# Expert layer of a routed feed-forward stage: second product with the expert's weights as the loaded operand, and a turn of its result on TensorE

## The reference

```python
def _L1_ffn_ref(hidden_states, gate_w, gate_b, w1, w3, w2):
    x = hidden_states.reshape(T, D)
    probs = jax.nn.softmax((x @ gate_w + gate_b).astype(jnp.float32), axis=-1)
    top_w, top_idx = jax.lax.top_k(probs, TOP_K)
    top_w = top_w / jnp.sum(top_w, axis=-1, keepdims=True)
    combine = combine.at[jnp.arange(T)[:, None], top_idx].set(top_w)
    h = jax.nn.silu(jnp.einsum('td,edf->tef', x, w1)) * jnp.einsum('td,edf->tef', x, w3)
    out_e = jnp.einsum('tef,efd->ted', h, w2)
    out = jnp.einsum('ted,te->td', out_e, combine)
```

## Time and profile before

| | us |
|---|---|
| three runs | 1422.41, 1417.07, 1421.33 |
| median | 1421.33 |
| profiled execution | 1421.32 |
| its span | 1419.4 |
| mean granted clock of TensorE | 0.896 of full speed |

### The profile page before, as it was taken

One profiled execution on the slowest core, in us unless ns is written; L12 is line 12 of the kernel. 1 busy time (PEld: TensorE's weight loads), 2 busy tenths in 40 slices (PEclk: granted clock), 3 DMA queues, 4 the chain that ended last, 5 costly groups with the idle time before them and its releaser, 6 DMA issues. The chain is left out here.

```text
span 1419.4 us, 16931 instructions
## 1 busy us (share of the span) xinstructions
PE 1132.3 (80%) x5006; PEld 565.5 (40%) x5006; DVE 1013.0 (71%) x1416; ACT 785.3 (55%) x1269; POOL 725.3 (51%) x611
## 2 busy tenths in 40 slices
PE   4664689999999888888898889896684678777764
PEld 1221234444444333333333333332233567566563
DVE  4996775666645379999999999999927545444454
ACT  5664545646554468676777768584343333333344
POOL 0122351323312038887978888877621465565554
PEclk8775899999999989999999999999986788888885
DMA  6000000000000001000000000000001011111214
GB/s 209 0 0 0 0 2 0 1 1 0 0 0 1 0 30 30 15 16 15 15 16 15 30 0 0 0 0 1 0 9 52 27 40 41 38 39 40 41 41 171
DMA packets 13849, 33.25 MB, mean 23 GB/s; under 512 B 3568, under 2 KB 3760, under 8 KB 13552
## 3 DMA queue, kind: packets, MB, share of 16 engines
q1 hardware_dynamic: 8784, 22.10, 4.7%
q0 software_dynamic: 4992, 10.23, 2.7%
HBM read 23.01 MB, written 9.31 MB: 23 GB/s over the span
## 5 line engine op out<-in xcount | busy, mean ns | idle before, releaser
L1617 POOL TENSOR_TENSOR prod<-hs,csb 128x1024 f32<-128x1024 f32 x128 | 302.0, 2360 | 179.4 <-DVE hs L1667 178.5
L1667 DVE TENSOR_TENSOR_SCAN hs<-dA,carry,pD 128x512 f32<-128x512 f32 x256 | 313.9, 1268 | 5.5 <-DVE pD L1682 0.8
L1425 PE MATMUL pY<-prod,const 128*128 128x512 f32 x512 | 245.2, 601 | 11.3 <-DVE h L1652 7.4
L1532 ACT ACTIVATE dA<-dt,negA 128x512 f32<-128x512 f32 x256 | 169.9, 715 | 1.4 <-DVE dt L1719 1.4
L2388 DVE SCALAR_TENSOR_TENSOR hid<-pR,silu 128x512 f32<-128x512 f32 x78 | 53.9, 691 | 136.3 <-ACT silu L2099 97.4
L1425 PEld LDWEIGHTS pY<-prod,const 128*128 128x128 f32 x512 | 96.5, 192 | 122.3 <-issue 107.7
L1543 ACT ACTIVATE csb<-pC 128x512 f32<-128x512 f32 x128 | 76.0, 594 | 108.2 <-PE pC L1438 107.9
L2165 POOL DMA_INDIRECT moe_outs<-y,to x78 | 82.0, 1052 | 91.9 <-ACT y L2091 76.0
L2099 ACT ACTIVATE silu<-pR 128x512 f32<-128x512 f32 x78 | 46.5, 596 | 132.3 <-remote 66.7
L2145 POOL DMA_INDIRECT g<-moe_rows,source x78 | 80.3, 1029 | 48.9 <-DVE source L2337 25.5
L1878 PE MATMUL pR<-x,moe_hi 128*128 128x256 f16 x312 | 94.8, 304 | 12.1 <-issue 5.7
(11 more groups left out here) (398 smaller groups left out, 2719.5 us busy)
## 6 DMA issues: line engine op xcount, KB each, us to landing
raw<-moe_w SPq DMA_DIRECT2D x12, 512.0 KB, 3.6
room<-moe_outs SPq DMA_DIRECT2D x8, 512.0 KB, 7.5
X<-xT SPq DMA_DIRECT2D x4, 512.0 KB, 4.6
hidw<-hid_w SPq DMA_DIRECT2D x1, 2048.0 KB, 10.0
moe_rows<-xt SPq DMA_DIRECT2D x8, 256.0 KB, 2.0
outT<-X SPq DMA_DIRECT2D x8, 256.0 KB, 2.0
g<-moe_rows,source POOLq DMA_INDIRECT x78
moe_outs<-y,to POOLq DMA_INDIRECT x78
```

Of the source, the lines that this page charges most:

```text
L1425: last = nc.tensor.matmul(YB[c][:], G.ident, prod[:, slot(b, n), c, :], start=n == 0, stop=n == DST - 1)
L1532: last = nc.scalar.activation(dA[:, slot(b, n), c, :], dt[:, b, c, :], ACT.Exp, scale=negA[:, c, n:n + 1])
L1617: nc.gpsimd.tensor_tensor(prod[:, slot(b, n), :, :], hs[:, slot(b, n), :, :], csb[:, slot(b, n), :, :].to_broadcast([P, CB, N]), ALU.mult)\
L1667: last = nc.vector.tensor_tensor_scan(hs[:, slot(b, n), c, :], dA[:, slot(b, n), c, :], dBu(n, c), carry[:, b, n, c:c + 1], ALU.mult, ALU.add)
```

## The change

`down` uses the helper `product`, with the expert's weights as the loaded operand and all 256 rows moving: 6 matmuls of 256 columns per unit where there were 12 of 128. The result has channels on partitions, in the lower half of the bank. ACT copies it with the scale 1/WS to a new tile `y_by_channel` of 32-bit numbers (`take_y`), PE turns it by two matmuls of 128 columns against the 32-bit identity into the upper half of the bank (`y_turn`), and ACT copies that to `y` (`put_y`). `take_y(i - 2)` stands where `put_y(i - 2)` stood; `y_turn(i - 2)` and `put_y(i - 2)` come one unit later, `y_turn` between `up` and `down`. The ring of gathered tiles is 6 in place of 8, with `AHEAD` still 6.

```diff
@@ down, on PE
                 for h in range(2):
                     m = slice((2 * u + h) * P, (2 * u + h + 1) * P)
-                    w_hi, w_lo = of_expert(w2_hi, e, m), of_expert(w2_lo, e, m)
-                    for r in range(2):
-                        out = Y[:, i % 2, r * P:(r + 1) * P]
-                        at = slice(h * ROWS + r * P, h * ROWS + (r + 1) * P)
-                        nc.tensor.matmul(out, hid_hi[:, n % HR, at], w_hi, start=u == 0 and h == 0 and r == 0, stop=False)
-                        nc.tensor.matmul(out, hid_hi[:, n % HR, at], w_lo, start=False, stop=False)
-                        last = nc.tensor.matmul(out, hid_lo[:, n % HR, at], w_hi,
-                                                start=False, stop=u == 1 and h == 1 and r == 1)
+                    at = slice(h * ROWS, (h + 1) * ROWS)
+                    last = product(Y[:, i % 2, 0:ROWS], of_expert(w2_hi, e, m), of_expert(w2_lo, e, m),
+                                   hid_hi[:, n % HR, at], hid_lo[:, n % HR, at], u == 0 and h == 0, u == 1 and h == 1)
                 last.then_inc(S["down"], 1)
+            def y_turn(i):
+                pe.wait_ge(S["y_in"], i + 1)
+                for r in range(2):
+                    last = nc.tensor.matmul(Y[:, i % 2, ROWS + r * P:ROWS + (r + 1) * P],
+                                            y_by_channel[:, i % 2, r * P:(r + 1) * P], G.ident, start=True, stop=True)
+                last.then_inc(S["y_turned"], 1)
@@ the loop on PE
+                if u == 1 and i >= 2:
+                    y_turn(i - 2)
                 if n >= LAG:
                     down(n - LAG, es[(n - LAG) // 2])
             for n in range(UNITS - LAG, UNITS):
                 down(n, es[n // 2])
+                if n == UNITS - 2:
+                    y_turn(TILES - 2)
+            y_turn(TILES - 1)
@@ ACT
+            def take_y(i):
+                act.wait_ge(S["down"], 2 * i + 2)
+                if i >= 2:
+                    act.wait_ge(S["y_turned"], i - 1)
+                nc.scalar.activation(y_by_channel[:, i % 2, :], Y[:, i % 2, 0:ROWS], ACT.Copy, scale=1.0 / WS)\
+                  .then_inc(S["y_in"], 1)
             def put_y(i):
-                act.wait_ge(S["down"], 2 * i + 2)
+                act.wait_ge(S["y_turned"], i + 1)
...
                 if u == 0 and i >= 2:
+                    take_y(i - 2)
+                if u == 1 and i >= 2:
                     put_y(i - 2)
             hid_high(UNITS - 1)
             act.preload_act_table_set("natural_log_exp_and_others")
-            put_y(TILES - 2)
-            put_y(TILES - 1)
+            for i in (TILES - 2, TILES - 1):
+                take_y(i)
+                put_y(i)
```

More of the change, by code:

```diff
@@ L1744, in phase_moe @@
     GRID = B * T // ROWS
-    AHEAD, GR, HR, YR = 6, 8, 4, 4
+    AHEAD, GR, HR, YR = 6, 6, 4, 4
     SOON, LATE = 16, COLS - 16
@@ L1815, in phase_moe @@
         y = sb("y4", [P, YR, 2, P])
+        y_by_channel = sb("y_by_channel4", [P, 2, ROWS])
         w13_hi, w13_lo = G.moe_hi[:, 0:E, :], G.moe_lo[:, 0:E, :]
@@ L1845, in phase_moe @@
                  "past expert_f expert hot_col hot_part hot_pair hot_low listed row_f empty second from_f to source "
-                 "gathered0 gathered1 gathered2 gathered3 gathered4 gathered5 gathered6 gathered7 scattered0 scattered1 scattered2 scattered3 x_turned x_in up silus hidden hid_high hid_low down y_out "
+                 "gathered0 gathered1 gathered2 gathered3 gathered4 gathered5 scattered0 scattered1 scattered2 scattered3 x_turned x_in up silus hidden hid_high hid_low down y_in y_turned y_out "
                  "back0 back1 back2 back3 back4 back5 back6 back7 summed minus squaredC weighted logC rstdC scale scaledC turnedC addedC stored").split()
@@ L2085, in hid_high @@
                 nc.scalar.activation(hid_hi[:, n % HR, :], hid[:, n % HR, :], ACT.Copy).then_inc(S["hid_high"], 1)
+            def take_y(i):
[4 more added lines that the diff above has]
+                  .then_inc(S["y_in"], 1)
             def put_y(i):
-                act.wait_ge(S["down"], 2 * i + 2)
+                act.wait_ge(S["y_turned"], i + 1)
                 if i >= YR:
                     act.wait_ge(S[f"scattered{i % YR}"], 32 * (i // YR))
-                nc.scalar.activation(y[:, i % YR, :, :].rearrange("p r d -> p (r d)"), Y[:, i % 2, 0:2 * P], ACT.Copy,
-                                     scale=1.0 / WS).then_inc(S["y_out"], 1)
+                nc.scalar.activation(y[:, i % YR, :, :].rearrange("p r d -> p (r d)"), Y[:, i % 2, ROWS:2 * ROWS], ACT.Copy)\
+                  .then_inc(S["y_out"], 1)
             for n in range(UNITS):
```

## The result

Six runs of the changed kernel have a median of 1433.57 us (1430.80 to 1436.04), six of the kernel before 1421.32 us (1417.07 to 1423.03). The ratio is 1.0089, 95% interval 1.0065 to 1.0113: slower by some 12 us where the forecast was 3 us faster. That is outside the forecast's own range of 1408 to 1428, though inside the wide one of 1378 to 1454, and of the three outcomes the prediction had given slower the largest chance, 0.41. The profiled execution took 1435.15 us, its span 1433.4.

A forecast was written before the change was run, and what follows sets the result against it. Bound taken: PE, starved of instructions while POOL issues indirect DMAs. Terms -9.6 (fewer instructions) + 3.8 (last six tiles) + 1.5 (wait) + 1.2 (end) = -3.1 us, from 1421.32 to 1418 us; own range 1408 to 1428, wide 1378 to 1454.

The forecast's parts named there:

- What bounds the kernel: Tile loop: while POOL issues indirect DMAs, PE gets instructions slowly, 4.9 a us once its reserve is gone.
- down at 0: PE's down: twelve matmuls of 256 columns take 1.32 us a tile, as 24 of 128 did; nothing won or lost.
- The turn at 0.64 us a tile: Two 32-bit matmuls a tile on PE: 0.64 us at a clock of 0.85, making an undisturbed tile 4.83 us.
- The last six tiles: End of the loop, without stalls: the added turn is paid in full, 6 x 0.64 = +3.8 us.
- Instructions, -9.6 us: PE in the 33 tiles with gathers: 112 instructions a tile for 128 shorten stalls, 0.29 us a tile, -9.6 us.
- The bound of "nothing at all": Lower bound on the gain from fewer PE instructions: none, if the stalls do not care about their number.
- The last tiles, the wait and the end, +6.5 us together: Turn in the last six tiles +3.8 us, PE's wait there for ACT's copy +1.5, kernel's end +1.2.
- wrong at the root: Sign against the forecast: PE stalls where POOL issues nothing, or PE's stalls move to waits for ACT.
- The ring of 6, put_y later, ACT's second copy: nothing: Gather ring, put_y one unit later, and ACT's extra 0.38 us copy a tile: all hidden, no cost.
- B: Rival, chance 0.38: stalls ignore the instruction count and the turn comes on top; 1451 us, tile of 7.5 us and more.
- A: Rival, chance 0.27 in full or part: stalls mostly go, POOL sets the loop's pace; 1377 us.

## Why the prediction failed

*What bounds the kernel.* Right for the 1421 kind: the stalls belong to POOL's runs of indirect DMAs (no gathers, or plain ones, and they are gone). That PE gets its instructions late there remains a reading: no run separates it from another cause of POOL's runs. That ACT is late in the same runs, which the copy at 1280.34 shows, was not in it.

*down at 0.* Right: 1.0000 and 1.0012 for the new down alone.

*The turn at 0.64 us a tile.* Too high. The undisturbed tile takes 4.60 us on either kind of chip, where 4.83 was said, and 4.15 with the new down alone: the turn costs 0.42 to 0.45. The 0.64 was the busy time of the records, and part of that overlaps with what follows: the turn at 1271.57 in the changed kernel lasts 0.65 us, and the next down begins 0.49 us after its start. The last six tiles would pay 2.5 us, not 3.8.

*Instructions, -9.6 us.* This is the step that failed. Its model was a fixed number of late instructions during POOL's run and a fixed rate after it. The new down alone has more than this relief (104 instructions a tile, the changed kernel 112) and none of the turn, and gives +1.7 us (-0.7 to +4.0). The bound of "nothing at all", which the prediction had named, is what was measured. The rate of 4.9 a us was one stretch's; there was no ground to apply it to a different stream. POOL's runs of eight became more, sixteen for ten, and the idle time went over to DVE's x or ACT's copy.

*The last tiles, the wait and the end, +6.5 us together.* Measured with the turn: 8.7 us on the 1421 kind. The end is +1.6 for +1.2. The wait was mis-sized in kind: sized from ACT's lateness in one undisturbed tile (0.5 us), it is 2.2 to 6.2 us in each run of eight DMAs. How much of that is net cost stays open: PE had stood in such runs before too. The prediction did say that PE's stalls moving to waits for ACT would prove it wrong at the root, and that is what the thirteen waits are.

*The ring of 6, put_y later, ACT's second copy: nothing.* In the changed kernel's trace POOL's gathers never wait for PE in the loop, so the ring cost nothing there. ACT's 77.5 of 199.7 us busy bear the rest out as to load, but the place of its first copy, behind a late silu, was not free: PE stood for it.

*The rivals.* B's mechanism (the stalls don't care about the count, and the turn comes on top) is the right one, at +10 to +12 us and not at +30. It was priced too high: 38 turns of 0.45 us are 17 us at full clock, and 8.7 were measured. That the rest is done in time that PE would have lost is a reading. A's regime exists, but on the other kind of chip, and gives no gain there, since that kind is at POOL's pace already before the change. The loop tile between 1150 and 1350 us, which was to be 6.6 us for the forecast and 7.5 and more for B, is 7.3.

With the relief at nothing, the prediction's own sum is +6.5 us, 1428: 0.5% slower, and within 6 us of what was measured. Part of that closeness is luck: its turn was sized too high, and its wait from one undisturbed tile.

No version that was run beats the kernel before and computes the whole.

## What to carry over

Where one engine's stream stands still while another issues, fewer instructions do not buy the time back; find what makes the stretch end, and price the change by that. A new dependency between two engines that are both held up in the same stretch makes one stand for the lateness of the other, here 2.2 to 6.2 us at a time, and not for the copy's 0.4 us. And where GpSimd's indirect DMAs set the pace, look at what VectorE has just begun when each of them is issued: moving PE's work by half a tile was worth 0.6% there.

## What the runs showed of the hardware

- Two kinds of chip for one program: 1420.84 us and 1361.96 to 1363.48 us. The new down alone has 254.7 us between first and last turn of x on the first kind, with idle time of PE in every run of eight DMAs, and 190.3 us on the second, where PE waits for gathered rows alone; that is the whole difference between its two times. Without the gathers PE runs without a gap, the kernel before on the second kind and the changed one on the first. What makes the chips differ was not found.
- An indirect DMA of 128 rows takes POOL 0.96 to 1.00 us, and 1.32 to 1.41 us when a DVE subtraction of two SBUF tiles has begun 0.12 to 0.23 us ahead of it. DVE's hid, with one input in PSUM, has no such effect: where only it was running at the DMA's start, none lasts over 1.00 us.
- On the 1421 kind ACT too starts late in such stretches, 2.49 us after its last work with its input there.
